# Cross-attention and a routed feed-forward: the context's key one group sooner, probabilities turned first, three heads divided on ScalarE

## The chip, the core and the metric

One core of one Trainium2 chip. The metric is the device time of one execution in microseconds (us).

## The reference

x is (8, 128, 256): 8 batch rows of 128 tokens. Each row goes through grouped attention with 16 query heads of width 128 over 4 key heads, with 128 context tokens put ahead of the row's own 128; then through a feed-forward with 8 experts, of which each token takes 2. Cut to the attention:

```python
q = rms_norm((x @ wq).reshape(B, L, 16, 128), q_norm_w)      # x here: layer-normed
k = rms_norm((x @ wk).reshape(B, L, 4, 128), k_norm_w)
k_ctx = rms_norm((h_ctx_kv @ wk_ctx).reshape(B, T, 4, 128), k_norm_w)   # no rotation
q = q * cos + rotate_half(q) * sin
k = k * cos + rotate_half(k) * sin
k_full = jnp.concatenate([k_ctx, k], axis=1)                  # values alike, without norm
probs = softmax(einsum('blhd,bmhd->bhlm', q, k_full) * scale + mask)
out = einsum('bhlm,bmhd->blhd', probs, v_full).reshape(B, L, 2048) @ wo
x = x + out
```

## The kernel before

The kernel walks over the 8 rows b, and inside a row over 4 groups g of 4 heads, one per key head. Row 0 and row 7 are written out, rows 1 to 6 are a hardware loop. Every engine has its own function `row(b, first, last)` with its instructions in an order written by hand; engines meet through semaphores only. A step number is u = 4b + g. `ahead_of(b, g, n, last)` names the group n steps later, over the row's end.

Each product is taken in three fp16 terms, so each operand is stored as a high half (ScalarE, `copy`, L471) and a low half (VectorE, `low`, L929): the tiles `..._hi` and `..._lo`. A step goes through the engines so:

- TensorE `scores` (L1318, L1340) into `sc_ps`; VectorE `scores_max` (L991) and the bias `nbias` (L995); ScalarE `exps` (L566) into `probs`; VectorE the reciprocal `rden` (L1000) and `normalise` (L1003), which divides the 4 heads one by one.
- One step later TensorE turns `probs` by 8 products (`turn_probs`, L1351) into `pt_ps`; ScalarE and VectorE make its halves (`p_copy`, `p_low`); TensorE multiplies by the values (`mix`, L1361) into `o_ps`; then `o_copy` and `o_low`.
- The query is made two groups ahead: TensorE `q` (L1203) into `proj`; VectorE rotates it (L920, L922); GpSimd adds the two parts into `q_rot` (`q_add`, L795) and makes the inverse root of its mean square (`q_roots`, L747 and L749) from ScalarE's `q_squares` (L510). One group ahead TensorE turns it (`q_turn`, L1297) into the bank `turn`, and `q_copy` and `q_low` make its halves.

In group 0 the context's value (`vc`) and the value (`v`, through `turn`) of the row are projected. In group 1 the row before gets its output projection (`out_proj`, L1388, 48 products into `proj[0]`) and its residual (`residual`, L1013). In group 2 the next row's context key (`kc`, L1216, into `turn`) and key (`k`, L1203, into `proj[1]`) are projected, ScalarE takes their squares (`kc_squares`, `k_squares`), GpSimd their roots (`kc_roots`, `k_roots`) and scales the key (`k_scale`, L781); ScalarE scales the context's key (`kc_scale`). In group 3 both are turned (L1249, L1268) and their halves are made, ScalarE's in the midst of the exponentials. The next row's scores need both high halves at their start and both low halves (`k_ready`, `kc_ready`) before their third part, the four products with `kT_lo`. The context of the next row is split by `ctx_high` and `ctx_low` in group 0 and turned by a DMA from SP's queue.

The bank `turn` is shared by the turned query, the value, the context's key and the turned context's key; each waits until the one before has been read.

Row 0 also prepares the output weights: in group 1 GpSimd multiplies half of them by a scale (L843) after its query's root; ScalarE and VectorE split them (`wo_split`).

## Time and profile before

| | us |
|---|---|
| median of 3 runs | 361.87 (359.09 to 362.88) |
| the profiled execution | 362.58 |
| its span, first to last instruction | 360.80 |
| mean granted TensorE clock | 0.982 of full |

Rows are in microseconds from the span's start. PE is TensorE's products, PEld its weight loads, DVE VectorE, ACT ScalarE, POOL GpSimd. A timeline row gives start, duration, engine, line, operation, names and shapes, the count merged into it, and in brackets how long the engine had been idle and what ended that. Products are pipelined, so their durations overlap and the step from start to start is what one costs. On the other engines the start of the next instruction comes a little before the end of the last.

### The profile page before, as it was taken

The numbers are of one execution on the slowest core, as the hardware profiler recorded it, in microseconds if no ns is written. First come the engines' busy times: TensorE is split into PE (matmuls) and PEld (weight loads), VectorE is DVE, ScalarE is ACT, GpSimd is POOL, SyncE is SP. The second block draws the span as 40 slices with busy tenths as digits, with TensorE's granted clock in tenths as the row PEclk, the third lists the DMA queues.
The fourth block names the chain that finished last, engine by engine and source line by source line (L and its number), as shares of the span: only waits on it lengthen the run. The fifth ranks groups of instructions, "written<-read, shape, count | busy, mean of one in ns | idle before, by whom it ended". The sixth has DMA issues, their size and how long they took to land.

```text
span 360.8 us, 7355 instructions
## 1 busy us (share of the span) xinstructions
PE 327.0 (91%) x2250; PEld 219.6 (61%) x2254; DVE 314.5 (87%) x602; ACT 259.9 (72%) x910; POOL 166.7 (46%) x241
## 2 busy tenths in 40 slices
PE   6677869779999999999999999999999999999994
PEld 5253635447665856585667566756766587856452
DVE  1578999989999899999998999899989997875773
ACT  4577769666898599759974997498759875747541
POOL 4366465854375427443734443454436431054530
PEclk9998989989999999999999999999999999999998
DMA  5996300002007100710031001000000000044683
GB/s 172 344 287 226 54 0 0 3 0 45 0 1 174 44 0 0 182 36 1 0 73 29 0 0 29 15 0 0 15 15 0 3 2 0 2 83 94 132 162 115
DMA packets 42450, 21.07 MB, mean 58 GB/s; under 512 B 31672, under 2 KB 39872, under 8 KB 42432
## 3 DMA queue, kind: packets, MB, share of 16 engines
q1 hardware_dynamic: 42432, 20.86, 22.7%
q8 instruction: 8, 0.13, 0.2%
q14 instruction: 10, 0.08, 0.1%
HBM read 12.20 MB, written 1.05 MB: 37 GB/s over the span
## 4 chain that ended last, share of the span: by engine, by line
PE 40%; DVE 19%; ACT 19%; issue 11%; POOL 6%; DMA 2%; SPq 1%; DVEq 1%; ACTq 0%; POOLq 0%
PE proj L1388 10%; ACT probs L566 8%; PE pt_ps L1351 6%; DVE probs L1003 4%; PE o_ps L1361 4%; PE proj L1203 4%; PE turn L1297 4%; POOL q_rot L795 3%; DVE nmax L991 3%; PE sc_ps L1318 3%; DVE pT_lo L929 2%; ACT pT_hi L471 2%; DMA wq<-in_L_xattn_wq_dram 2%; ACT kc_junk L510 2%; ACT q_junk L510 2%
## 5 line engine op out<-in xcount | busy, mean ns | idle before, releaser
L566 ACT ACTIVATE probs<-sc_ps,nbias,q_r 128x256 f32<-128x256 f32 x128 | 71.0, 574 | 6.5 <-DVE nbias L995 6.0
L795 POOL TENSOR_TENSOR q_rot<-q_t 128x512 f32<-128x512 f32 x32 | 42.4, 1325 | 42.6 <-DVE q_t L922 41.8
L1003 DVE TENSOR_SCALAR probs<-probs,rden 128x256 f32<-128x256 f32 x128 | 51.0, 460 | 1.1
L510 ACT ACTIVATE q_junk<-proj 128x128 bf16<-128x128 f32 x128 | 34.3, 304 | 12.9 <-DVE q_t L922 12.9
L1203 PE MATMUL proj<-wq_hi,xT 128*128 128x512 f16 x128 | 39.0, 387 | 3.8 <-DVE wq_lo L913 3.4
L471 ACT ACTIVATE pT_hi<-pt_ps 128x512 f16<-128x512 f32 x64 | 34.8, 598 | 9.2 <-PE pt_ps L1351 9.2
L929 DVE SCALAR_TENSOR_TENSOR pT_lo<-pt_ps,pT_hi 128x512 f16<-128x512 f32 x64 | 40.9, 680 | 0.2 <-ACT pT_hi L471 0.2
L991 DVE TENSOR_REDUCE nmax<-sc_ps 128x4 f32<-128x1024 f32 x32 | 38.9, 1214 | 1.5 <-PE sc_ps L1340 1.5
L749 POOL TENSOR_TENSOR q_r<-q_me,power 128x4 f32<-128x4 f32 x32 | 34.5, 1077 | 2.5
L1351 PE MATMUL pt_ps<-ident,probs 128*128 128x128 f32 x256 | 33.3, 273 | 0.4 <-DVE probs L1003 0.3
L471 ACT ACTIVATE qT_hi<-turn 128x512 f16<-128x512 f32 x32 | 19.6, 613 | 18.2 <-PE turn L1297 18.2
L471 ACT ACTIVATE oT_hi<-o_ps 128x512 f16<-128x512 f32 x32 | 19.9, 621 | 16.9 <-PE o_ps L1361 16.9
L1388 PE MATMUL proj<-wo_lo,oT_hi 128*128 128x256 f16 x112 | 30.5, 273 | 0.0
L1388 PE MATMUL proj<-wo_hi,oT_hi 128*128 128x256 f16 x112 | 30.5, 273 | 0.0
L1388 PE MATMUL proj<-wo_hi,oT_lo 128*128 128x256 f16 x112 | 30.5, 273 | 0.0
L1351 PEld LDWEIGHTS pt_ps<-ident,probs 128*128 128x128 f32 x256 | 28.8, 141 | 1.1 <-DVE probs L1003 0.9
L510 ACT ACTIVATION_READ_ACCUMULATOR q_junk<-proj 128x1 f32 x128 | 29.3, 236 | 0.0
L1361 PE MATMUL o_ps<-pT_hi,v_hi 128*128 128x512 f16 x64 | 24.3, 380 | 4.8 <-DVE pT_lo L929 4.7
L1297 PE MATMUL turn<-ident,q_rot 128*128 128x128 f32 x128 | 20.0, 279 | 8.9 <-POOL q_rot L795 6.2
L566 ACT ACTIVATION_READ_ACCUMULATOR probs<-sc_ps,nbias,q_r 128x1 f32 x128 | 27.5, 215 | 0.0
L929 DVE SCALAR_TENSOR_TENSOR oT_lo<-o_ps,oT_hi 128x512 f16<-128x512 f32 x32 | 22.0, 686 | 5.3 <-ACT oT_hi L471 5.3
L1318 PE MATMUL sc_ps<-kT_hi,qT_hi 128*128 128x256 f16 x128 | 24.5, 273 | 0.9 <-ACT probs L566 0.5
(216 smaller groups left out, 866.2 us busy)
## 6 DMA issues: line engine op xcount, KB each, us to landing
wq<-in_L_xattn_wq_dram SPq DMA_DIRECT2D x4, 512.0 KB, 9.1
w<-in_L_ffn_w_dram SPq DMA_DIRECT2D x2, 1024.0 KB, 10.4
wq<-in_L_xattn_wo_dram SPq DMA_DIRECT2D x1, 2048.0 KB, 8.1
ctx_b<-in_ctx_dram SPq DMA_DIRECT2D x8, 128.0 KB, 2.3
out_dram<-x_all SPq DMA_DIRECT2D x4, 256.0 KB, 2.2
x_all<-in_x_dram SPq DMA_DIRECT2D x1, 896.0 KB, 12.4
wkc<-in_L_xattn_wk_ctx_dram SPq DMA_DIRECT2D x1, 512.0 KB, 4.4
wk<-in_L_xattn_wk_dram SPq DMA_DIRECT2D x1, 512.0 KB, 5.3
```

The lines of the kernel that those rows point to most:

```text
L471: return nc.scalar.activation(out_, in_, ACT.Copy, scale=scale)
L510: last = nc.scalar.activation(junk[:, head], bank[:, head], ACT.Square, scale=scale, accum_out=dst[:, h:h + 1])
L566: last = nc.scalar.activation(probs[:, h, :], sc_ps[:, h, :], ACT.Exp, bias=nbias[:, h:h + 1], scale=q_r[:, g, h:h + 1], accum_out=den[:, ...
L795: nc.gpsimd.tensor_tensor(q_rot[:], q_t1[:], q_t2[:], ALU.add).then_inc(q_added, 1)
L929: return nc.vector.scalar_tensor_tensor(out=lo, in0=src, scalar=scale, in1=hi, op0=ALU.mult, op1=ALU.subtract)
L991: nc.vector.tensor_reduce(nmax[:], sc_ps[:], AX_X, ALU.max, negate=True).then_inc(s_max, 1)
L1003: last = nc.vector.tensor_scalar(probs[:, h, :], probs[:, h, :], rden[:, h:h + 1], None, ALU.mult)
L1203: last = nc.tensor.matmul(bank[:], xT[:, a, c, :], w[:, c, cols], start=(n == 0), stop=(n == 3 * DC - 1))
L1318: nc.tensor.matmul(sc_ps[:, h, :], a[:, h * P:(h + 1) * P], w[:, g, :, :].rearrange("p a t -> p (a t)"), start=start, stop=False, skip_gro ...
L1351: last = nc.tensor.transpose(pt_ps[:, a, h * P:(h + 1) * P], probs[:, h, a * P:(a + 1) * P], ident[:])
L1361: last = nc.tensor.matmul(o_ps[:], v[:, a, g * P:(g + 1) * P], p[:, a, :], start=(a == 0 and i == 0), stop=(a == 1 and i == 2))
L1388: last = nc.tensor.matmul(proj[0][:, 0:D], o[:, h // R, (h % R) * P:(h % R + 1) * P], w[:, h, :], start=(h == 0 and i == 0), stop=(h == H ...
```

## The change

1. `kc(b + 1)`, the next row's context key, is issued by TensorE in the middle of the output projection of group 1 (in row 0: at the end of group 1), instead of in group 2. ScalarE's `kc_squares` and GpSimd's `kc_roots` move into group 1; `kc_scale` stands first in group 2. The query's turn of group 3 waits for the scaled context key (`kc_norm`); that of group 0 no longer does.
2. In groups 1 and 2 TensorE turns the probabilities ahead of the query; ScalarE and VectorE make the halves in the same order. In groups 0 and 3 the order stays.
3. `by_act = (1, 2, 0, 0)`: ScalarE divides the last head in group 0 and the last two in group 1 (`normalise_rest`), VectorE the others. `turn_probs` waits for both.
4. ScalarE's and VectorE's halves of the context's value and of the next context come earlier in group 0.
5. On GpSimd, `q_roots` of the next row's first query follows its `q_add` at once, ahead of `k_roots`; `q_add` in group 2 no longer has `kc_roots` ahead of it.

```diff
@@ -356,8 +357,13 @@
         shared_banks = (o_ps[:], turn[:])
         gate_ps = (proj[1][:, 0:TT * E], turn[:, 0:TT * E])
         xn2_banks = (proj[1][:], turn[:], sc_a, sc_b)
+        by_act = (1, 2, 0, 0)
         half_e = (slice(0, E // 2), slice(E // 2, E))
         wT_landed = 16 * 3 * len(half_e)
+
+        def act_normalised(b, g):
+
+            return 2 * b + g
 
         def token_turned(eng, k):
 
@@ -569,6 +575,13 @@
                         last.then_inc(s_exp_half, 1)
                 last.then_inc(s_exp, 1)
 
+            def normalise_rest(b, g):
+                u = G * b + g
+                act.wait_ge(s_rden, u + 1)
+                for h in range(R - by_act[g], R):
+                    last = copy(probs[:, h, :], probs[:, h, :], rden[:, h:h + 1])
+                last.then_inc(s_probs_act, 1)
+
             def p_copy(u):
                 act.wait_ge(p_turned, u + 1)
                 for a in range(2):
@@ -620,19 +633,29 @@
             def row(b, first, last):
                 for g in range(G):
                     u = G * b + g
-                    if ahead_of(b, g, 1, last):
+                    if g in (0, 3) and ahead_of(b, g, 1, last):
                         q_copy(*ahead_of(b, g, 1, last))
                     if g == 1 and first:
                         ln_high(b + 1)
+                    if g == 2 and not last:
+                        kc_scale(b + 1)
                     if g or not first:
                         p_copy(u - 1)
+                    if g in (1, 2):
+                        q_copy(b, g + 1)
                     exps(b, g, (kc_copy, k_copy) if g == 3 and not last else ())
                     if g == 1 and not first and not last:
                         ln_high(b + 1)
-                    if g == 2 and not last:
-                        kc_squares(b + 1)
+                    if g == 0:
+                        vc_copy(b)
+                    if g == 0 and not last:
+                        ctx_high(b + 1)
                     if ahead_of(b, g, 2, last):
                         q_squares(*ahead_of(b, g, 2, last))
+                    if g == 1 and not last:
+                        kc_squares(b + 1)
+                    if by_act[g]:
+                        normalise_rest(b, g)
                     if first and g == 3:
                         wo_split(3)
                     if g == 0:
@@ -640,17 +663,12 @@
                     if (g or not first) and not (g == 3 and last):
                         o_copy(u - 1, (g - 1) % G)
                     if g == 2 and not last:
-                        kc_scale(b + 1)
                         k_squares(b + 1)
                     if g == 2 and last:
                         act.wait_ge(t_sh2, 1)
                         copy(gateT[:].rearrange("p c e -> p (c e)"), proj[0][:, D:D + DC * E])
                         copy(sh2T[:], proj[0][:, 0:D]).then_inc(r_sh2, 1)
                         xn_copy(1)
-                    if g == 0:
-                        vc_copy(b)
-                    if g == 0 and not last:
-                        ctx_high(b + 1)
                     if first and g == 1:
                         wo_split(0)
                         wo_split(1)
@@ -823,13 +841,12 @@
                         q_add(*ahead_of(b, g, 2, last))
                     if g == 0 and first:
                         ln_root(b + 1)
-                    if g == 2 and not last:
-                        kc_roots(b + 1)
                     if ahead_of(b, g, 2, last):
                         if g in (1, 2) and not first:
                             q_add(*ahead_of(b, g, 2, last))
-                        if g != 2:
-                            q_roots(*ahead_of(b, g, 2, last))
+                        if g == 1 and not last:
+                            kc_roots(b + 1)
+                        q_roots(*ahead_of(b, g, 2, last))
                     if g == 0 and not first and not last:
                         ln_root(b + 1)
                     if g == 1 and not first:
@@ -837,7 +854,6 @@
                     if g == 2 and not last:
                         k_roots(b + 1)
                         k_scale(b + 1)
-                        q_roots(b + 1, 0)
                     if first and g == 1:
                         pool.wait_ge(d_wo, 16)
                         nc.gpsimd.tensor_tensor(wo32[:, own_wo, :], wo32[:, own_wo, :],
@@ -999,7 +1015,7 @@
                 dve.wait_ge(s_exp, u + 1)
                 nc.vector.reciprocal(rden[:], den[:]).then_inc(s_rden, 1)
                 dve.wait_ge(s_rden, u + 1)
-                for h in range(R):
+                for h in range(R - by_act[g]):
                     last = nc.vector.tensor_scalar(probs[:, h, :], probs[:, h, :], rden[:, h:h + 1], None, ALU.mult)
                 last.then_inc(s_probs, 1)
 
@@ -1060,12 +1076,14 @@
                         wo_split(0)
                     if first and g == 0:
                         split_low(wv32[:], wv_hi[:], wv_lo[:], G + 2)
-                    if ahead_of(b, g, 1, last):
+                    if g in (0, 3) and ahead_of(b, g, 1, last):
                         q_low(*ahead_of(b, g, 1, last))
+                    if g or not first:
+                        p_low(u - 1)
+                    if g in (1, 2):
+                        q_low(b, g + 1)
                     if g == 1 and not first and not last:
                         ln_scale(b + 1)
-                    if g or not first:
-                        p_low(u - 1)
                     if g == 2 and not first:
                         second_norm(b - 1)
                     if ahead_of(b, g, 2, last):
@@ -1091,14 +1109,13 @@
                         wc_split(1)
                     if g == 0:
                         v_low(b)
+                        vc_low(b)
+                    if g == 0 and not last:
+                        ctx_low(b + 1)
                     if g or not first:
                         o_low(u - 1, (g - 1) % G)
                     if g == 2 and not last:
                         k_add(b + 1)
-                    if g == 0:
-                        vc_low(b)
-                    if g == 0 and not last:
-                        ctx_low(b + 1)
 
             row(0, True, False)
             with dve.Fori(1, B - 1) as b:
@@ -1236,7 +1253,7 @@
                     pe.wait_ge(cT_ready, 1)
                 else:
                     pe.wait_ge(d_cT, 16 * nb)
-                    pe.wait_ge(q_ready, G * nb)
+                    pe.wait_ge(q_ready, G * nb - 1)
                     pe.wait_ge(wc_low, 1)
                 project_ctx(nb, turn, wkc, wkc_hi, wkc_lo, kc_proj)
 
@@ -1284,15 +1301,18 @@
             def q_turn(b, g, last=False):
                 pe.wait_ge(q_added, G * b + g + 1)
                 if g == 0:
-                    pe.wait_ge(kc_norm, b + 1)
                     if isinstance(b, int) and b == 0:
                         pe.wait_ge(kc_ready, 1)
+                    else:
+                        pe.wait_ge(q_ready, G * b)
                 if g == 1:
                     pe.wait_ge(kc_ready, b + 1)
                 if g == 2:
                     pe.wait_ge(v_ready, b + 1)
                 if g == 3:
                     pe.wait_ge(q_ready, G * b + g)
+                    if not last:
+                        pe.wait_ge(kc_norm, b + 2)
                 for h in range(R):
                     last_ = nc.tensor.transpose(turn[:, h * P:(h + 1) * P], q_rot[:, h * P:(h + 1) * P], ident[:])
                 last_.then_inc(q_turned, 1)
@@ -1345,6 +1365,8 @@
 
                 u = G * b + g - 1
                 pe.wait_ge(s_probs, u + 1)
+                if by_act[(g - 1) % G]:
+                    pe.wait_ge(s_probs_act, act_normalised(b, g))
                 seen(pe, p_ready, 2 * u)
                 for a in range(2):
                     for h in range(R):
@@ -1376,12 +1398,14 @@
                 if g == G - 1:
                     last.then_inc(wo_done, 1)
 
-            def out_proj(b):
+            def out_proj(b, final):
                 pe.wait_ge(o_ready, G * b + G - 1)
                 pe.wait_ge(q_sq, G * b + G + 3)
                 pe.wait_ge(wo_low2, 1)
                 pe.wait_ge(wo_low, 2)
                 for h in range(H):
+                    if h == H // 2 and not final:
+                        kc(b + 2)
                     if h == H - R:
                         pe.wait_ge(o_ready, G * b + G)
                     for i, (o, w) in enumerate(((oT_hi, wo_hi), (oT_hi, wo_lo), (oT_lo, wo_hi))):
@@ -1455,10 +1479,12 @@
                 for g in range(G):
                     u = G * b + g
                     scores(b, g)
-                    if ahead_of(b, g, 1, last):
+                    if g in (0, 3) and ahead_of(b, g, 1, last):
                         q_turn(*ahead_of(b, g, 1, last), last)
                     if g or not first:
                         turn_probs(b, g)
+                    if g in (1, 2):
+                        q_turn(b, g + 1, last)
                     if first and g < 2:
                         pe.wait_ge(w_lo, g + 4)
                     if ahead_of(b, g, 2, last):
@@ -1467,7 +1493,6 @@
                         kc_turn(b + 1)
                         k_turn(b + 1)
                     if g == 2 and not last:
-                        kc(b + 1)
                         k(b + 1)
                     if g == 0:
                         vc(b)
@@ -1478,7 +1503,9 @@
                         v(b)
                     if g == 1:
                         if not first:
-                            out_proj(b - 1)
+                            out_proj(b - 1, last)
+                        else:
+                            kc(1)
                         pe.wait_ge(vc_ready, b + 1)
                         pe.wait_ge(v_ready, b + 1)
                     if g == 2 and last:
```

## Rows read from the trace of the kernel before

**Rows 1.** Part 1 of the page: busy time, share of the span, instructions.
```profile
PE 327.0 (91%) x2250; PEld 219.6 (61%) x2254; DVE 314.5 (87%) x602; ACT 259.9 (72%) x910; POOL 166.7 (46%) x241
```
**Rows 2.** Busy time per stretch; this one is one row of the loop.
```profile
core 0: us, PE busy (x) PEld busy (x) DVE busy (x) ACT busy (x) POOL busy (x), PEclk, DMA share, GB/s
...
183.19:218.27 35.08, 33.76 (x241) 23.34 (x240) 33.69 (x68) 27.81 (x108) 15.77 (x24) 1.00 0.05 11
```
**Rows 3.** Timeline of TensorE in that row: start, duration, what, idle before.
```profile
184.67 0.22 PE L1340 MATMUL sc_ps<-causal,identb 128*128 128x128 bf16 x1
185.37 0.63 PE L1297 MATMUL turn<-ident,q_rot 128*128 128x128 f32 x4 [0.48 <-DVE v_lo L929]
...
188.00 0.27 PE L1388 MATMUL proj<-wo_hi,oT_hi 128*128 128x256 f16 x1
...
193.24 0.38 PE L1361 MATMUL o_ps<-pT_hi,v_hi 128*128 128x512 f16 x1
...
194.53 0.38 PE L1318 MATMUL sc_ps<-kT_hi,qT_hi 128*128 128x256 f16 x2
...
198.68 1.46 PE L1216 MATMUL turn<-wk,cT 128*128 128x512 f16 x6
199.97 0.59 PE L1203 MATMUL proj<-wk_hi,xT 128*128 128x512 f16 x2
...
204.80 0.65 PE L1297 MATMUL turn<-ident,q_rot 128*128 128x128 f32 x4 [0.54 <-POOL q_rot L795]
...
208.29 0.66 PE L1268 MATMUL proj<-ident,k_rot 128*128 128x128 f32 x4 [0.24 <-POOL k_rot L781]
...
211.19 0.27 PE L1318 MATMUL sc_ps<-kT_lo,qT_hi 128*128 128x256 f16 x1
```
**Rows 4.** Timeline of VectorE in the same row.
```profile
186.68 1.21 DVE L991 TENSOR_REDUCE nmax<-sc_ps 128x4 f32<-128x1024 f32 x1
...
191.51 2.21 DVE L1003 TENSOR_SCALAR probs<-probs,rden 128x256 f32<-128x256 f32 x4
...
195.36 0.69 DVE L929 SCALAR_TENSOR_TENSOR oT_lo<-o_ps,oT_hi 128x512 f16<-128x512 f32 x1 [0.50 <-ACT oT_hi L471]
196.27 1.22 DVE L991 TENSOR_REDUCE nmax<-sc_ps 128x4 f32<-128x1024 f32 x1 [0.21 <-PE sc_ps L1340]
...
201.14 1.14 DVE L1003 TENSOR_SCALAR probs<-probs,rden 128x256 f32<-128x256 f32 x4
...
204.04 1.17 DVE L980 TENSOR_TENSOR k_sum<-k_t 128x512 f32<-128x512 f32 x1
205.14 1.21 DVE L991 TENSOR_REDUCE nmax<-sc_ps 128x4 f32<-128x1024 f32 x1
...
210.12 0.68 DVE L929 SCALAR_TENSOR_TENSOR kT_lo<-proj,kT_hi 128x512 f16<-128x512 f32 x1
```
**Rows 5.** Timeline of ScalarE: a probability copy and an exponential of group 2.
```profile
197.58 0.60 ACT L471 ACTIVATE pT_hi<-pt_ps 128x512 f16<-128x512 f32 x1 [0.28 <-PE pt_ps L1351]
...
198.55 0.57 ACT L566 ACTIVATE probs<-sc_ps,nbias,q_r 128x256 f32<-128x256 f32 x1
```
**Rows 6.** Timeline of GpSimd: the rotated query, in groups 1 and 2.
```profile
191.51 1.27 POOL L795 TENSOR_TENSOR q_rot<-q_t 128x512 f32<-128x512 f32 x1
...
203.40 1.26 POOL L795 TENSOR_TENSOR q_rot<-q_t 128x512 f32<-128x512 f32 x1
```
**Rows 7.** Timeline of GpSimd in row 0, groups 1 and 2.
```profile
46.20 4.26 POOL L843 TENSOR_TENSOR wq<-wq,scale_w 128x2048 f32<-128x2048 f32 x1
53.54 1.26 POOL L795 TENSOR_TENSOR q_rot<-q_t 128x512 f32<-128x512 f32 x1 [3.09 <-DVE q_t L922]
```
**Rows 8.** Timeline of VectorE in row 0, group 2.
```profile
48.76 1.71 DVE L995 TENSOR_TENSOR nbias<-nmax,q_r 128x4 f32<-128x4 f32 x1
...
53.58 2.16 DVE L1003 TENSOR_SCALAR probs<-probs,rden 128x256 f32<-128x256 f32 x4
```
**Rows 9.** Timeline of TensorE: row 0 group 2, and the last row.
```profile
51.17 2.72 PE L1216 MATMUL turn<-wk,cT 128*128 128x512 f16 x6 [2.87 <-issue]
...
290.44 0.63 PE L1297 MATMUL turn<-ident,q_rot 128*128 128x128 f32 x4 [0.23 <-DVE v_lo L929]
```

More of the change, by code:

```diff
@@ L305, in xattn_moe_kernel @@
         s_probs = sem("s_probs")
+        s_probs_act = sem("s_probs_act")
         p_turned = sem("p_turned")
```

## The prediction

> **What bounds the kernel now.** I read the page's busy shares first [rows 1]: TensorE is busy for 91% of the span and VectorE for 87%, so neither share names the limit. Next came the busy time of one whole row of the loop [rows 2]. Of its 35.08 us TensorE is busy for 33.76, VectorE for 33.69 and ScalarE for 27.81. There are six such rows. Two engines that are both nearly full hand the lead to each other, so the rest is read from timelines: who waits for whom, and at which place.
>
> TensorE [rows 3]: it runs from the first scores of group 1 (183.19) to those of group 2 (194.53) with one stall. Scores end at 184.73, 0.06 after the row of 184.67, and the query's turn starts at 185.37, held by VectorE's v_lo: 0.64 idle. In groups 2 and 3 it stalls three times more: about 0.7 ahead of the turn at 204.80 (0.54 by the row, which counts from a modelled end), 0.4 ahead of the key's turn at 208.29, and some 0.2 inside the next scores.
>
> VectorE [rows 4]: it idles where group 1 ends, 0.50 for the output's high half and 0.21 for the scores of group 2. From the maximum at 196.27 to the key's low half (210.12, ending at 210.80) it works almost without a break: 14.53 us. TensorE needs that low half for the third part of the next scores, which starts at 211.19, so VectorE has 0.39 to spare there. The row is therefore a loop of two legs. **TensorE's leg** goes from the third part of scores 0 to the end of scores 2. **VectorE's leg** goes from the maximum of group 2 to the key's low half. TensorE's stalls of groups 2 and 3 lie beside VectorE's leg and are not lost time.
>
> **The change, part by part, in a loop row.** (1) *The context's key moves from group 2 into the output projection of group 1.* It is 6 products, 198.68 to 199.97: 1.29 us [rows 3]. It leaves group 2, where TensorE has room, and enters TensorE's leg: +1.29. I expect no stall ahead of it. It would start at 184.73 + 0.87 + 0.44 + 1.30 + 2.62 = 189.96 (turned probabilities, turned query, projection, half of the output projection of 188.00 to 193.24). The low half of the query that it waits for comes by about 189.9: the maximum of group 1 at 186.68 as before, 1.34 to the bias, two probability halves (1.21) and 0.60. The margin is about zero, so 0 to 0.3 per row stays in the range. The transfer of the turned context starts about 0.7 earlier than before, since its split is moved ahead.
>
> (2) *Probabilities are turned ahead of the query.* They don't need v_lo, and VectorE's division ends before the scores do. The 0.64 goes: −0.64. TensorE's leg thus changes by 1.29 − 0.64 = **+0.65**.
>
> (3) *ScalarE divides 1 head of group 0 and 2 of group 1.* VectorE saves 3 x 0.27, a quarter of the free division of four heads at 201.14 (1.14 with its tail, [rows 4]). But in group 0 its next step waits for ScalarE's v_hi, which is queued behind the moved copy and the division, and in group 1 it already idles for TensorE. So the saving ends as more idle time. What ScalarE needs for one the trace doesn't show: between 0.3 (half of its 512-wide copy of 0.60) and 0.57 (its exponential of the same 256 columns) [rows 5]. I take 0.38, as a copy does no sum, 1.1 in all. ScalarE is idle for 7.3 us of the row [rows 2], and the turns that wait for its last head come some 2 us later. I take 0 for both.
>
> (4) *GpSimd adds the rotated query of group 2 at once, instead of behind the key's mean square.* This is the costly edit. Before, GpSimd held q_rot until 203.40, where it made k_sum wait: k_sum took 1.10 from start to start against 0.60 when alone [rows 4, 6]. Now q_rot starts as soon as the second half of the rotation is there, and so does the division, one reciprocal later. Wherever the two start together, the division's four heads take 2.21 instead of 1.14 (at 191.51) [rows 4, 6]. Row 0 of the kernel already has this very order in group 2: q_rot at 53.54, division at 53.58 for 2.16 [rows 7, 8]. So +1.07 for the division, −0.50 for k_sum. VectorE now takes the probabilities' low half ahead of the query's, 1.34 after the maximum; ScalarE's high half of it starts 0.2 (the maximum's own lag behind the scores) less than 0.87 + 0.2 after that maximum and takes 0.60 (the copy at 197.58, [rows 5]), so it is there at 1.5 and VectorE waits: +0.20. Sum of VectorE's leg: 1.07 − 0.50 + 0.20 = **+0.77**.
>
> The Trainium skill (SBUF — State Buffer, "SBUF: two separate sides") says that GpSimd and a VectorE instruction of this kind share a port pair which "starts first gets the pair for the whole instruction". The waits of 1.07 agree. By that rule alone it would matter who is first: if the division won all four times, it would lose nothing and the sum would be 1.07 per row less. That is a rival below.
>
> A loop row changes by 0.65 + 0.77 less the 0.39 to spare: **+1.03**. Six rows: +6.2. A check by VectorE's own time: 35.08 less 0.71 idle is 34.37 of work, waits for GpSimd in it; less 0.81 and plus 0.57 that is 34.1. It leaves some 2.0 idle at the end of group 1: the 0.71 of before, 0.65 for TensorE's longer leg, 0.54 for the two heads that it no longer divides there. 36.1 against 35.1.
>
> **Row 0.** There the context's key is projected at the end of group 1 at about 43.5, once its input has been turned and the low half of query 2 is there. ScalarE's squares of it then end at 46.5 to 47.3. GpSimd takes the key's root (1.35) and then the query's (1.25) ahead of its scaling of the output weights, which before started at 46.20 and took 4.26 [rows 7]. It starts at 49.2 to 50.1 now and ends at 53.4 to 54.3. Before, its end held up VectorE's bias, 1.71 instead of 0.16, until 50.47 [rows 8]. The maximum would end at about 50 to 50.8, inside the scaling, so the bias would wait until its end: +3.0 to +3.8. TensorE's idle time ahead of the context's key (2.87, [rows 9]) goes, but VectorE's chain runs beside it. I take +3.0. If the bias slips in before the scaling starts, it is −1.6 instead.
>
> **Last row.** No context key; the query's turn at 290.44 stood 0.39 idle: −0.4.
>
> **Sum.** 6.2 + 3.0 − 0.4 = +8.8. The profiled execution took 362.58 (span 360.80), so 371.4 for it; it lies 0.7 above the median of the runs, 361.87, from which the same sum gives **370.7**.
>
> **Rivals.** *The division wins the port (18%).* q_rot starts by 0.04 us first in row 0 [rows 7, 8] and at the same 10 ns in the loop; a shift of a few hundredths would turn it round, though a head alone is 0.27 and q_rot could still come between two. Then VectorE's leg changes by −0.30, and the row by 0.65 − 0.30 − 0.39, about 0. With row 0 and the last: 361.87 + 2.6 = 364.5.
>
> *Row 0 does not lose (10%).* The bias gets through ahead of the scaling. The sum is 6.2 − 1.6 − 0.4: 366.1.
>
> *VectorE's work doesn't end the loop (10%), faster.* If TensorE alone sets the row, all four stalls (0.64 + 0.70 + 0.40 + 0.23) could go, but VectorE's 34.1 of work stops it at −1.0 per row: 361.87 − 6.0 − 0.4 = 355.5. It decides from the point at which VectorE's leg is under 14.53 + 0.39 − 0.65 = 14.27 us. For it speak the stalls that the moved normalisation removes; against it, that VectorE works those 14.53 us with no gap to close, and that none of the moved divisions lies in it.
>
> *The change does nothing that lasts (10%).* The parts cancel: the leg of VectorE keeps its length, the moved key is paid by the stall that goes. 361 to 364.
>
> **Numbers.** Forecast 52% (368 to 373). The bounds of the unknown costs are 0 to 0.3 per row for the wait ahead of the moved key, −1.07 to 0 for the port, −1.6 to +3.8 in row 0. The range takes in the two middle rivals: 364 to 373.5. About 1% is what a measurement of this kernel can tell from no change. Slower by over 1% (above 365.5): the forecast, the second rival and under half of the first, 0.70. Within 1%: the rest of the first and nearly all of the last, 0.19. Faster: the third and a little of the last, 0.11.
>
> **What would show it.** In the profile after: a loop row of about 36.1 (35.08 before); six more products inside the output projection, and the mix behind it ending some 0.65 later against the scores of group 1; VectorE idle for about 2 us in group 1, with its wait for the output projection as a new line; the first head of the division in group 2 at about 1.4 us instead of 0.35, q_rot beside it; k_sum at 0.7 instead of 1.17; TensorE waiting for k_lo or k_rot in group 3. In row 0, the bias of group 2 ends at 53 or later. The forecast is wrong if the maximum of group 2 to the key's low half takes no longer than 14.3 us, or if VectorE doesn't idle at the end of group 1.

## The result, and the profile after

| | before | after |
|---|---|---|
| median of 6 runs, us | 361.48 (359.09 to 362.88) | 373.98 (371.65 to 374.73) |
| the profiled execution | 362.58 | 374.73 |
| its span | 360.84 | 373.01 |

The ratio is 1.037, interval 1.033 to 1.041: 12.5 us slower. The forecast was slower too, by 8.8 us: 370.7 in a range that ended at 373.5, half a microsecond under the measured median.

I cut the span at the starts of VectorE's maximum of group 0, one per row. "A loop row" below is the distance of two such starts, as read for row 5 unless said otherwise; the medians of the runs stand beside it.

| part of the span, us | before | after | difference | forecast |
|---|---|---|---|---|
| start to row 0 | 28.73 | 28.36 | −0.37 | 0 |
| row 0 | 39.70 | 42.00 | +2.30 | +3.0 |
| row 1 | 39.09 | 39.72 | +0.63 | +1.03 |
| rows 2 to 6 | 175.49 | 184.43 | +8.94 | +5.2 |
| row 7 and the end | 77.82 | 78.50 | +0.68 | −0.4 |

So the five steady rows hold nearly all that was missed. The busy time of one of them (the windows view; columns as in [rows 2]):

```profile
220.72:257.62 36.90, 34.76 (x243) 22.95 (x242) 33.58 (x65) 28.95 (x110) 15.90 (x24) 1.00 0.05 11
```

The row is 36.90 long where [rows 2] had 35.08. VectorE is busy for 33.58 of it (33.69 before), so it now idles 3.32 where it idled 1.39. TensorE has the same products; its busy time, whose ends are modelled, is 1.00 longer. TensorE's timeline of that row, where the moves can be seen:

```profile
229.10 0.63 PE L1317 MATMUL turn<-ident,q_rot 128*128 128x128 f32 x4
229.61 0.60 PE L1220 MATMUL proj<-wq_hi,xT 128*128 128x512 f16 x2
...
233.43 0.27 PE L1412 MATMUL proj<-wo_hi,oT_lo 128*128 128x256 f16 x1
233.71 1.47 PE L1233 MATMUL turn<-wk,cT 128*128 128x512 f16 x6
235.02 0.27 PE L1412 MATMUL proj<-wo_hi,oT_hi 128*128 128x256 f16 x1
...
250.36 0.61 PE L1220 MATMUL proj<-wq_hi,xT 128*128 128x512 f16 x2 [1.27 <-ACT k_junk L516]
252.25 0.66 PE L1266 MATMUL turn<-ident,kc_n 128*128 128x128 f32 x4 [0.42 <-DVE qT_lo L945]
```

The context's key stands in the middle of the output projection: 233.71 to 235.02 is 1.31, and 0.17 of waiting lies ahead of it (0.28 from the start of the product before it, which costs 0.11). In group 2, which the context key's products have left, TensorE now idles 1.27 until ScalarE has taken the squares of the key; that place lies beside VectorE's leg. VectorE's timeline:

```profile
225.74 1.52 DVE L1019 TENSOR_SCALAR probs<-probs,rden 128x256 f32<-128x256 f32 x3
...
228.26 0.69 DVE L945 SCALAR_TENSOR_TENSOR v_lo<-turn,v_hi 128x512 f16<-128x512 f32 x1 [0.92 <-ACT v_hi L477]
228.87 0.68 DVE L945 SCALAR_TENSOR_TENSOR v_lo<-proj,v_hi 128x512 f16<-128x512 f32 x1
...
237.96 0.42 DVE L1029 SCALAR_TENSOR_TENSOR x_all<-proj,x_all 128x256 f32 x1 [1.03 <-PE proj L1412]
...
239.76 0.69 DVE L945 SCALAR_TENSOR_TENSOR oT_lo<-o_ps,oT_hi 128x512 f16<-128x512 f32 x1 [0.56 <-ACT oT_hi L477]
240.67 1.23 DVE L1007 TENSOR_REDUCE nmax<-sc_ps 128x4 f32<-128x1024 f32 x1 [0.21 <-PE sc_ps L1360]
...
242.18 1.29 DVE L945 SCALAR_TENSOR_TENSOR pT_lo<-pt_ps,pT_hi 128x512 f16<-128x512 f32 x2
...
245.70 2.17 DVE L1019 TENSOR_SCALAR probs<-probs,rden 128x256 f32<-128x256 f32 x4
...
249.58 0.68 DVE L996 TENSOR_TENSOR k_sum<-k_t 128x512 f32<-128x512 f32 x1
```

Three things answer to [rows 4]. The division of group 2 takes 2.17 where it took 1.14, and GpSimd's q_rot starts 0.04 ahead of it:

```profile
245.66 1.27 POOL L813 TENSOR_TENSOR q_rot<-q_t 128x512 f32<-128x512 f32 x1 [4.78 <-DVE q_t L938]
```

k_sum takes 0.68 instead of 1.17. And at the end of group 1 VectorE idles 1.80 in three pieces (1.03, 0.56, 0.21), the first of them new. What the prediction had not put a price on is the 0.92 ahead of v_lo. ScalarE's timeline tells where it is from:

```profile
225.41 0.60 ACT L477 ACTIVATE v_hi<-proj 128x512 f16<-128x512 f32 x1 [0.67 <-PE o_ps L1383]
225.91 0.41 ACT L477 ACTIVATE cT<-ctx_b 128x256 f16<-128x256 f32 x1
226.21 0.27 ACT L516 ACTIVATE q_junk<-proj 128x128 bf16<-128x128 f32 x1
...
227.21 0.53 ACT L477 ACTIVATE probs<-probs,rden 128x256 f32<-128x256 f32 x1
227.61 0.62 ACT L477 ACTIVATE v_hi<-turn 128x512 f16<-128x512 f32 x1
```

The moved copy of the context's value may not overwrite v_hi before the mix has read it, so it waits 0.67 with the query's squares, the division and the value's own copy queued behind it.

In lengths of the two legs of the prediction, row 5: TensorE's leg 19.96 before and 21.46 after, VectorE's 14.52 and 15.18, VectorE's spare time ahead of the third part of the scores 0.40 and 0.06. 1.50 + 0.66 − 0.34 = 1.82, which is the 36.90 − 35.08. The spare time is what the legs leave of a row, with 0.2 from the end of scores 2 to VectorE's maximum; where it grows, something other than VectorE holds the next scores.

### The profile page after: what moved, and what is told of

Its sections match the earlier page's. It is cut to its first block and busy times, and to the rows that moved or that the text cites. A ratio compares the mean times of both kernels' runs of the same rounds, so it can differ in the third digit from the quotient of the medians.

```text
span 373.0 us, 7378 instructions
## 1 busy us (share of the span) xinstructions
PE 332.5 (89%) x2254; PEld 217.6 (58%) x2254; DVE 313.2 (84%) x578; ACT 269.1 (72%) x934; POOL 166.6 (45%) x241
## 5 line engine op out<-in xcount | busy, mean ns | idle before, releaser
L767 POOL TENSOR_TENSOR q_r<-q_me,power 128x4 f32<-128x4 f32 x32 | 33.5, 1045 | 2.5
L1373 PEld LDWEIGHTS pt_ps<-ident,probs 128*128 128x128 f32 x256 | 27.5, 141 | 5.2 <-issue 4.3
L1383 PE MATMUL o_ps<-pT_hi,v_hi 128*128 128x512 f16 x64 | 25.2, 394 | 2.8 <-DVE pT_lo L945 2.8
L516 ACT ACTIVATION_READ_ACCUMULATOR q_junk<-proj 128x1 f32 x128 | 27.6, 216 | 0.0
L1383 PE MATMUL o_ps<-pT_lo,v_hi 128*128 128x512 f16 x64 | 25.3, 395 | 0.0
L1383 PE MATMUL o_ps<-pT_hi,v_lo 128*128 128x512 f16 x64 | 25.3, 395 | 0.0
```

What stands on the lines that cost most here:

```text
L516: last = nc.scalar.activation(junk[:, head], bank[:, head], ACT.Square, scale=scale, accum_out=dst[:, h:h + 1])
L1373: last = nc.tensor.transpose(pt_ps[:, a, h * P:(h + 1) * P], probs[:, h, a * P:(a + 1) * P], ident[:])
L1383: last = nc.tensor.matmul(o_ps[:], v[:, a, g * P:(g + 1) * P], p[:, a, :], start=(a == 0 and i == 0), stop=(a == 1 and i == 2))
```

## The experiments

All kernels are before or after with parts put in or taken out. One table for the outcomes; every ratio is against runs of before on the same chip.

| kernel | median, us | ratio (interval) | loop row | TensorE's leg | VectorE's leg |
|---|---|---|---|---|---|
| before | 361.5 | | 35.08 | 19.96 | 14.52 |
| after | 373.98 | 1.037 (1.033 to 1.041) | 36.90 | 21.46 | 15.18 |
| a_kcback: after, key in its old place | 365.66 | 1.015 (1.007 to 1.023) | 35.68 | 19.70 | 15.20 |
| a_nodiv: after, ScalarE divides none | 369.38 | 1.028 (1.020 to 1.037) | 36.49 | 21.06 | 15.17 |
| a_oldg0: after, group 0 in the old order | 370.39 | 1.029 (1.021 to 1.037) | 36.38 | 20.95 | 15.17 |
| a_kturn: after, key rotated ahead of the division | 370.63 | 1.030 (1.022 to 1.038) | 36.59 | 21.45 | 14.88 |
| b_kc: before, key moved | 373.33 | 1.031 (1.028 to 1.035) | 37.02 | 21.33 | 15.40 |
| b_tp: before, probabilities first | 367.28 | 1.016 (1.011 to 1.021) | 35.77 | 19.75 | 15.20 |
| b_tp1: the same in group 1 alone | 358.75 | 0.991 (0.988 to 0.994) | 34.87 | 19.74 | 14.53 |
| a_both: key moved, probabilities first | 367.89 | 1.018 (1.014 to 1.021) | 36.53 | 21.10 | 15.18 |
| c_p34: before, division and order of group 0 | 365.16 | 1.015 (1.009 to 1.021) | 35.63 | 20.51 | 14.52 |
| c_vc: b_tp1, value's halves together | 356.81 | 0.986 (0.980 to 0.993) | 34.51 | 19.37 | 14.53 |
| c_vc_d2: and 1 head of group 2 on ScalarE | 358.00 | 0.995 (0.992 to 0.999) | 34.75 | 19.37 | 14.57 |
| c_vc_d12: and 2 of group 1 | 357.53 | 0.993 (0.990 to 0.996) | 34.71 | 19.37 | 14.55 |

The row is the surer column: from row 2 on it repeats within 0.1 us inside an execution, where the medians carry 2 to 3 us of row 0 (last section). Each row comes from one profiled execution. c_vc's median has the widest runs behind it, 353.0 to 359.9.

### Parts taken out of after

**a_kcback.**

```diff
+        if g == 2 and not last: kc(b + 1)   # TensorE, group 2
-        if h == H // 2 and not final: kc(b + 2)      # in the output projection
```

The cut shows TensorE's lines alone; ScalarE's squares and scaling, GpSimd's roots and the waits go back to group 2 with them.

> The changed kernel with the context's key, its squares, its root and its scaling back in group 2 (GpSimd's order there is that of before too); the turned probabilities first, the divisions on ScalarE and the earlier halves in group 0 stay. Theory A (the moved key costs 1.29 us on TensorE's leg, the collision of the division of group 2 with q_rot 0.5 on VectorE's): the loop row falls from 36.9 to 34.8 to 35.1, total 359 to 362. Rival B (the divisions and copies moved on ScalarE delay the value and set the row): the row stays at 36 or more, total over 368.

365.66 us. The loop row falls by 1.22 to 35.68: the moved key is most of the loss in a row. But the row is not that of before, as my theory had it, nor the 36 of the rival; there is something else that costs 0.6. b_tp below finds it.

**a_nodiv.**

```diff
-        by_act = (1, 2, 0, 0)
+        by_act = (0, 0, 0, 0)
```

> The changed kernel with by_act all zero: VectorE divides all heads, all else is as changed. Theory A: the value's high half comes 0.4 us earlier in group 0 (one division of 0.40 less ahead of it), which takes away up to 0.4 of TensorE's waits in group 1, and VectorE's 0.27 more per head falls into its idle time: row 36.4 to 36.8, total 371 to 374. Rival B: row under 36, total under 368.

The row falls by 0.41, all of it in TensorE's leg, as expected; the median of 369.38 is under the 371 to 374. In the profiled execution row 0 is 3.0 shorter than after's, which the theory had left out. ScalarE's division, costed at nothing, costs here, where it stands behind the moved copy and ahead of the value's copy. A division itself takes ScalarE 0.40, from 227.21 to the next start at 227.61 above.

**a_oldg0.**

```diff
+                    if g == 0:
+                        vc_copy(b)                   # ScalarE: behind v_copy and o_copy again
-                        vc_low(b)                    # VectorE: behind o_low again
```

The cut shows one line for each engine; both halves of the context's value, and the next context's with them, go back on both.

> The changed kernel with the halves of the context's value and of the next context back at the end of group 0, on ScalarE and VectorE. Theory A: ScalarE's copy of the context's value waits for the mix of the step before, and pushes the query's squares from 0.7 to 1.7 us behind the rotation and the value's high half with them. Back in its place it gives up to 0.4 per row (0.24 ahead of the query's turn, 0.17 ahead of the context's key): row 36.4 to 36.6, total 370.5 to 372.5. Rival B: row under 36. If the order was harmless: row 36.9, 374.

The row falls by 0.52, in TensorE's leg alone, just under the 36.4 to 36.6. Yet taking both out (a_both) leaves 36.53, no less than either alone: TensorE's leg is 21.10 with neither, 21.06 with the new order alone, 20.95 with the division alone, and 21.46 with both. With the key moved and the probabilities first, neither part costs anything by itself; together their delays of the value's high half add up, the wait for the mix and then the division. And even both together cost nothing with the probabilities first and the key in group 2: a_kcback is b_tp with parts 3 and 4, and its row is 35.68 against 35.77. So their price belongs to the combination: 0.55 on before (c_p34), 0 on b_tp, 0.36 on a_both. The query's product behind the turn starts 8.57 behind the maximum of group 0 in a_nodiv, 8.58 in a_oldg0 and 8.89 in after.

**a_kturn.**

```diff
+                    if g == 2 and not last: k_turn(b + 1)     # VectorE, two rotations
                     normalise(b, g)
-                    if g == 2 and not last: k_turn(b + 1)
```

> The changed kernel with VectorE's rotation of the key ahead of the division in group 2, so that q_rot on GpSimd is done before the division starts. Theory A: the division takes 1.14 instead of 2.17 and the key's squares come 2 us earlier; VectorE's leg gets 0.9 to 1.0 shorter and so does the row: 35.9 to 36.1, total 367.5 to 369.5. Rival C (TensorE alone sets the row since the key was moved): row stays at 36.8 or more, 373 to 374.

VectorE's leg falls by only 0.30 and the row by 0.31, between my theory and the rival. VectorE's timeline and GpSimd's:

```profile
244.08 1.15 DVE L1015 TENSOR_SCALAR probs<-probs,rden 128x256 f32<-128x256 f32 x4
...
247.60 0.88 DVE L1007 TENSOR_TENSOR nbias<-nmax,q_r 128x4 f32<-128x4 f32 x1
```

```profile
242.85 1.27 POOL L809 TENSOR_TENSOR q_rot<-q_t 128x512 f32<-128x512 f32 x1 [4.80 <-DVE q_t L934]
...
247.42 1.04 POOL L795 TENSOR_TENSOR k_rot<-k_sum,k_r 128x512 f32<-128x512 f32 x1
```

The 1.02 of the division goes, which shows that the collision with q_rot was the whole of it. But 0.72 comes back at once in the bias, which now meets k_rot: it starts 0.18 after it and ends with it (0.88 where it takes 0.16). The Trainium skill (SBUF — State Buffer, "SBUF: two separate sides") has the engine that comes first hold the shared port pair for its whole instruction. These rows agree: an instruction of 128 x 4 elements waited for one of 128 x 512.

### Parts added to before

**b_kc.** The key's move alone, GpSimd's order with it.

```diff
+                    if h == H // 2 and not final: kc(b + 2)
-                        kc(b + 1)
```

Again TensorE's lines alone.

> The kernel before with the context's key alone moved into group 1 (with its squares, root and scaling, and GpSimd's earlier q_add and root of group 2 that follow from it); the query is still turned first, no head on ScalarE, group 0 as before. Theory A: 1.29 on TensorE's leg and 0.5 on VectorE's, less the 0.4 that VectorE had to spare: row 36.4 to 36.6 (35.1 before), and row 0 over 2 us longer: total 370 to 373, about the whole loss. Rival D (the loss needs the moved order of turned probabilities or the divisions): row under 35.8, total under 366.

373.33 us, ratio 1.031: this edit alone costs nearly as much as the whole change, and in a row of the loop more (37.02 against 36.90; I had expected 36.4 to 36.6). It puts +1.37 on TensorE's leg (its six products take 1.29 to 1.31) and +0.88 on VectorE's. The long division and VectorE's new wait for the output projection are there in full:

```profile
234.69 2.19 DVE L1002 TENSOR_SCALAR probs<-probs,rden 128x256 f32<-128x256 f32 x4
238.03 0.42 DVE L1012 SCALAR_TENSOR_TENSOR x_all<-proj,x_all 128x256 f32 x1 [1.15 <-PE proj L1392]
...
246.00 2.16 DVE L1002 TENSOR_SCALAR probs<-probs,rden 128x256 f32<-128x256 f32 x4
```

The division and k_sum make 0.54 of VectorE's 0.88. The other 0.34 has no term in the prediction. The query's turn of group 3 writes into `turn`, where the projected context key now lies until ScalarE has scaled it. The turn starts 0.14 behind the maximum of group 2, where before had it 0.20 ahead; both halves of the query and of the probabilities move with it:

```profile
240.88 0.66 PE L1299 MATMUL turn<-ident,q_rot 128*128 128x128 f32 x4 [0.18 <-ACT kc_n L471]
```

**b_tp.** Probabilities ahead of the query in groups 1 and 2, on all three engines (TensorE's lines are shown).

```diff
-                    if ahead_of(b, g, 1, last):
+                    if g in (0, 3) and ahead_of(b, g, 1, last):
                         q_turn(*ahead_of(b, g, 1, last), last)
                     if g or not first: turn_probs(b, g)
+                    if g in (1, 2): q_turn(b, g + 1, last)
```

> The kernel before with the probabilities turned ahead of the query in groups 1 and 2, nothing else. Theory A: TensorE's 0.6 of group 1 goes; but in group 2 the context's key now waits for the query's low half, which VectorE makes 1.2 later, about 1.1 of idle on TensorE, and in the last row the turn of the normed tokens waits alike: row 34.8 to 35.2, total 360 to 362.5. Rival E (turning probabilities first is a plain gain): row 34.5, total 358 or less.

A loop row of 35.77 and a median of 367.28, longer than before and outside both expectations. TensorE's leg is 0.21 shorter, but in group 2:

```profile
235.97 0.68 DVE L931 SCALAR_TENSOR_TENSOR qT_lo<-turn,qT_hi 128x512 f16<-128x512 f32 x1
```

```profile
236.75 1.46 PE L1220 MATMUL turn<-wk,cT 128*128 128x512 f16 x6 [0.92 <-issue]
```

The context's key writes into the bank `turn`, and there it waits for the query's low half, which now comes behind the probabilities'. The key, its squares and its scaling come later, ScalarE's copy of the output behind them, and VectorE's leg is 0.68 longer. The spare time grows by 0.22 as well, since the key's turn has to wait for GpSimd's k_rot. This is the 0.6 left over in a_kcback, which has the same legs. Added to before, part 2 costs 0.69; added to b_kc it takes 0.49 off the row (a_both, 36.53), 0.23 on TensorE's leg and 0.22 on VectorE's, where it hides b_kc's wait for the scaled key. So in group 2 it seems worth having only where the key isn't there; b_kc with group 1 alone swapped was not run.

**b_tp1.** The same with `g in (1,)`.

> The kernel before with the probabilities turned ahead of the query in group 1 only, where the value's low half holds the query. Theory A: the stall of 0.6 on TensorE's leg goes and nothing waits in group 2: row 34.4 to 34.6, total 357.5 to 359, faster than before. Rival F (VectorE's total work of 34.4 sets the row, not the leg): row 34.9 to 35.1, total 361.

34.87, the first that beats before: ratio 0.991. It lies between my theory and the rival F. The stall of 0.64 ahead of the query's turn is gone, yet the row is only 0.21 shorter. What is late next:

```profile
217.71 0.60 PE L1301 MATMUL turn<-ident,q_rot 128*128 128x128 f32 x4
218.51 0.60 PE L1207 MATMUL proj<-wq_hi,xT 128*128 128x512 f16 x2 [0.20 <-DVE v_lo L931]
```

```profile
217.18 0.68 DVE L931 SCALAR_TENSOR_TENSOR oT_lo<-o_ps,oT_hi 128x512 f16<-128x512 f32 x1
217.78 0.68 DVE L931 SCALAR_TENSOR_TENSOR v_lo<-proj,v_hi 128x512 f16<-128x512 f32 x1
```

The next product of the query goes into the bank that holds the context's value, and waits until VectorE has made its low half (217.78 + 0.68 = 218.46). From the turn's start to the product's it is 0.80 where four turns cost 0.44: 0.36 of the 0.64 is back. Rival F falls with c_vc below, where the row drops to 34.51 with no work taken from VectorE.

**a_both.** After without parts 3 and 4, or: b_kc and b_tp together.

> The changed kernel without the divisions on ScalarE and with the halves of group 0 in their old places: the moved key and the turned probabilities alone. Theory A: all of TensorE's waits behind ScalarE's queue in group 0 are gone, and the row is what the prediction's sum for the key and the turn gives, 36.1 to 36.3; total 368 to 370. If the two undone edits add up (0.4 and 0.5): 36.0.

A row of 36.53, over the 36.1 to 36.3 that I expected. Against b_kc TensorE's leg is 0.23 shorter: part 2 is worth 0.2 here as in b_tp1, not 0.64. Against after it is 0.36 shorter: that is what parts 3 and 4 cost in this change. The places: in after the query's product starts 8.89 behind the maximum of group 0 (229.61 − 220.72), in a_both 8.71, and a_both has none of the 0.17 ahead of the key.

**c_p34.** Parts 3 and 4 alone on before.

> The kernel before with the other two parts of the change alone: ScalarE divides one head of group 0 and two of group 1, and in group 0 the context value's copy and the context's halves stand ahead of the query's squares (ScalarE) and ahead of the output's low half (VectorE). The context's key and the order of the turns stay as before. Theory (these two parts delay the value's halves, since the context value's copy waits for the mix ahead of the squares): the value's low half comes some 0.7 us later in a row than before, and the turn of the query, which waits for it, with it: a loop row of 35.7 to 36.0 us where before has 35.1, a ratio of 1.010 to 1.02, 365 to 369 us where before has 361.5. Rival (they cost nothing, as the prediction had it): a row of 35.0 to 35.2 us, 360 to 362.5 us.

A row of 35.63, 0.55 longer, just under what I expected; the rival of no cost is out. Where the query's turn still stands first, the whole delay falls on it:

```profile
219.70 0.69 DVE L940 SCALAR_TENSOR_TENSOR v_lo<-turn,v_hi 128x512 f16<-128x512 f32 x1 [0.70 <-ACT v_hi L473]
```

```profile
220.54 0.63 PE L1307 MATMUL turn<-ident,q_rot 128*128 128x128 f32 x4 [0.95 <-DVE v_lo L940]
```

1.11 of stall by the starts, where [rows 3] had 0.64.

### A version faster than both

**c_vc.** b_tp1, and the context value's halves right behind the value's on both engines. Part 4 of the change moved this copy too, but ahead of the squares, where it waits 0.67 for the mix; here it stands behind the value's copy and waits for nothing.

```diff
 ScalarE                    if g == 0:
                                v_copy(b)
+                               vc_copy(b)
 VectorE                    if g == 0:
                                v_low(b)
+                               vc_low(b)
                            if g or not first:
                                o_low(u - 1, (g - 1) % G)
```

> The kernel before with the probabilities turned first in group 1 only, and in group 0 the context value's high and low half made right behind the value's own, ahead of the output's halves (on ScalarE and on VectorE). Theory (with the turns swapped in group 1 alone, the next product of the query waits 0.36 us for the context value's low half, and this order gives it back): row 34.4 to 34.6 us where the swap alone has 34.87 and before 35.1; ratio 0.980 to 0.989, 355 to 357.5 us where before has 361.5. Rival (the output's low half, now later, holds up the output projection, or VectorE is what ends group 1): row 34.8 to 34.95, 358 to 359.5 us.

```profile
216.17 0.67 DVE L930 SCALAR_TENSOR_TENSOR v_lo<-proj,v_hi 128x512 f16<-128x512 f32 x1
216.76 0.67 DVE L930 SCALAR_TENSOR_TENSOR oT_lo<-o_ps,oT_hi 128x512 f16<-128x512 f32 x1
```

```profile
216.70 0.60 PE L1299 MATMUL turn<-ident,q_rot 128*128 128x128 f32 x4
217.13 0.59 PE L1205 MATMUL proj<-wq_hi,xT 128*128 128x512 f16 x2
```

The product now follows the turn with no wait (0.43), as expected. The row is 34.51, down by 0.36 from b_tp1 and by 0.57 from before, and the median 356.81, ratio 0.986. The output projection, for which the output's low half now comes 0.6 later, doesn't wait.

**c_vc_d2**, `by_act = (0, 0, 1, 0)`, and **c_vc_d12**, `by_act = (0, 2, 1, 0)`, on top of it:

> As the kernel with the context value's halves sooner, and ScalarE divides one head of four in group 2, where VectorE's leg (maximum of group 2 to the key's low half) stands between the key's rotation and its end. Theory (VectorE's leg sets the second half of the row, and loses one division of 0.3 us): row 34.1 to 34.3 us, 353.5 to 356 us. Rival (ScalarE's head delays the scaling of the context's key and the key's squares, which stand behind it, and so the key's turn): row 34.5 to 34.9 us, 356.5 to 359.5 us.

> As the one before, and ScalarE divides two heads of group 1 as well, where it is idle some 1.9 us and VectorE's first head meets GpSimd's sum of the query (2.16 us for four heads). Theory (in group 1 TensorE's leg is the one that ends last, so VectorE's shorter division moves nothing): the same row as with one head of group 2 alone, within 0.1 us. Rival (once the stall of group 1 is gone VectorE ends it): 0.1 to 0.4 us a row shorter than with one head of group 2 alone.

The rival held for the head of group 2. In c_vc_d2 VectorE's division is 0.26 shorter, but VectorE then waits for ScalarE, whose copy of the output stands behind its own head, and its leg ends no sooner (14.57 against 14.53):

```profile
231.83 0.88 DVE L1015 TENSOR_SCALAR probs<-probs,rden 128x256 f32<-128x256 f32 x3
...
234.53 0.69 DVE L941 SCALAR_TENSOR_TENSOR oT_lo<-o_ps,oT_hi 128x512 f16<-128x512 f32 x1 [0.62 <-ACT oT_hi L473]
```

The row is 0.24 longer than without, and VectorE's spare time takes most of that (0.62 where c_vc has 0.40). What comes late is the key's turn, 12.30 behind the maximum of group 2 where c_vc has 12.03, and the next scores with it. GpSimd's mean square of the key waits for ScalarE's squares, which stand behind ScalarE's own head, and k_rot waits for that:

```profile
239.25 0.66 PE L1281 MATMUL proj<-ident,k_rot 128*128 128x128 f32 x4 [0.41 <-POOL k_rot L793]
```

Two heads of group 1 change 0.04, as expected: VectorE is not the one who ends that group.

## Why the prediction missed

The direction, the two legs, the cost of the moved key and the collision of the division with q_rot were right. What failed is the sum of TensorE's leg, at two steps: "The 0.64 goes" for part 2, and "I take 0 for both" for parts 3 and 4. Together they make 0.77 of the 0.79 that a row came out too long.

- **TensorE's leg, +0.65 forecast, +1.50 measured.** The moved key was right: +1.29 forecast, +1.37 measured (b_kc), of which some 1.3 are its products. The 0.17 of waiting ahead of it in after lay in the 0 to 0.3 that was left open; a_both has none of it, so it belongs to parts 3 and 4. The prediction had worked out its margin of zero with the maximum of group 1 "as before"; it came 9.68 behind that of group 0 (230.40 − 220.72), where before has 8.91.
- **Part 2, −0.64 forecast, −0.23 measured** (a_both against b_kc). The step "They don't need v_lo, and VectorE's division ends before the scores do. The 0.64 goes" was right about that stall and stopped there. It didn't ask what is late next: the query's product behind it needs the context value's low half, 0.36 later (b_tp1; c_vc takes it away).
- **Parts 3 and 4, "I take 0 for both", +0.36 measured** (after against a_both; +0.55 alone in c_p34). The price of one head, 0.38 forecast and 0.40 measured, was right, as was that VectorE's saving ends as idle time. The step that failed is that nothing hangs on that idle time. VectorE's 0.92 stands ahead of v_lo, and three things on TensorE come late one behind the other: the query's turn waits for v_lo (228.26 + 0.69), its product for the context value's low half (228.87 + 0.68), and the moved key for the query's low half, which VectorE makes behind them. The prediction named v_lo as the holder of TensorE's stall in its first part, saw that v_hi is queued behind the moved copy and the division, and didn't join the two. Nor does it say that the moved copy waits for the mix. The 0.36 is the price in this change and not one of the parts: with the key in group 2 and the probabilities first it is 0 (a_kcback against b_tp).
- **VectorE's leg, +0.77 forecast, +0.66 measured.** Division +1.03 (forecast +1.07), k_sum −0.49 (−0.50). The leg's further term, the low half of the probabilities first, came out near the forecast +0.20: from the maximum to the query's rotation it is 3.63 in after and 3.47 in c_vc, which has the old order there. The spare time of 0.39 was used up but for 0.06. The forecast was near in part because part 2 is there: without it the moved key costs this leg 0.34 more (b_kc), which the prediction had not seen.
- **The rival of the port** didn't come: q_rot started 0.04 ahead of the division, the same small lead as in row 0 of before. In a_kturn, where the two don't meet, the gain of 1.02 was real and 0.72 of it was lost to the next collision.
- **Row 0, +3.0 forecast, +2.30 measured.** The bias of group 2 started at 50.30 and ended at 53.05, behind GpSimd's scaling of the output weights, as the prediction had it. The scaling started at 49.43, inside the forecast 49.2 to 50.1, but took 3.60 and not the 4.26 of [rows 7], so it ended at 53.03 and not at 53.4 to 54.3:

```profile
50.30 2.75 DVE L1011 TENSOR_TENSOR nbias<-nmax,q_r 128x4 f32<-128x4 f32 x1
```

```profile
49.43 3.60 POOL L859 TENSOR_TENSOR wq<-wq,scale_w 128x2048 f32<-128x2048 f32 x1
```

- **Last row, −0.4 forecast, +0.68 measured.** The change also turns the order of the halves in the last row's group 2, and there a turn of the normed rows into the bank `turn` waits for the query's low half, which now comes second. Before has no such wait at that place. b_tp has this order too and b_tp1 not, and from row 7 to the end b_tp takes 78.33 and b_tp1 77.60. The stall of 0.39 that was to go gave 0.2 (77.60 against 77.82), as in the rows of the loop.

```profile
316.04 0.65 PE L1438 MATMUL turn<-ident,xn_all 128*128 128x128 f32 x4 [1.15 <-DVE qT_lo L945]
```

- **The account.** Rows 1 to 6 brought 3.4 more than forecast, the last row 1.1 more, row 0 0.7 less and the start 0.4 less: 3.4, the distance from +8.8 to the +12.2 of the spans. Of the 0.79 that row 5 brought more, part 2 makes 0.41 on TensorE's leg, parts 3 and 4 0.36, and the three small ones (the key +0.08, VectorE's leg −0.11, the spare time +0.05) 0.02. This goes by legs in after. Built up part by part the shares are others, since the parts act on each other: the key alone costs 1.94 and not 1.47 (1.29 + 1.07 − 0.50 − 0.39), and part 2 on top gives back 0.49, near the forecast −0.64 + 0.20.
- **"Parts cancel", "row 0 does not lose"** didn't come. In a_nodiv the bias did get through, ahead of the scaling that started at 49.05, and row 0 took 39.02:

```profile
48.44 0.16 DVE L996 TENSOR_TENSOR nbias<-nmax,q_r 128x4 f32<-128x4 f32 x1
```

That its edit did this is not shown: in after the granted clock was 0.50 from 44.5 to 47.5, right ahead of that place, and in a_nodiv it was 1.00 there.
- **The signs that it had named for being wrong** didn't come either: VectorE's leg is 15.18, not under 14.3, and VectorE idles 1.80 at the end of group 1 (forecast about 2). Both look at VectorE, and the miss lies in TensorE's leg.

What stays open: row 1 grew by 0.63 only, against 1.8 in the rows behind it. It differs from them in every kernel (39.1 before) and I didn't take it apart. Some 1.6 of its length can be clock: the granted clock of row 1 is 0.96 in before and after and 1.00 in a_kturn and c_vc_d12, where row 1 takes 38.16 and 37.53. That doesn't explain the 0.63, as before and after have the same. How much of a kernel's row 0 is its order and how much its clock is open too (next section).

## What to carry to other kernels

When a stall goes, the gain is the distance to the next thing that is late there, so list what the next two instructions of that engine wait for before booking it: here 0.64 was worth 0.2 until the second wait was moved as well, and then 0.57. Work moved to an engine with idle time is free only if what is queued behind it, and releases the critical engine, can still come later: 0.4 of division on a ScalarE with 7 idle microseconds cost 0.4 of the row where the value's copy behind it was late already (after against a_nodiv), and nothing where it wasn't (a_oldg0 against a_both). So measure such a part in the combination in which it will run. And room in an engine's queue belongs to a place: TensorE had time for the context's key in group 2 and none in group 1.

## What the runs showed of the hardware

A GpSimd instruction with its operands in SBUF held up a small VectorE instruction that came behind it until it was done: the bias of 128 x 4 elements, 0.16 alone, took 2.75 beside the scaling of 128 x 2048 and 0.88 beside k_rot. Not every instruction is held: in before the output's low half, which reads a PSUM bank, took 0.69 at 203.43, inside q_rot's 203.40 to 204.66. A move of order took 1.02 off the division and put 0.72 on the next such instruction (a_kturn).

TensorE's granted clock fell to the lower of its two levels (1.2 instead of 2.4 GHz, a granted 0.50) at different places in kernels with the same code up to there. In before it is 0.50 from 31.0 to 33.5, just behind 1.96 of idle time ahead of the query's turn that opens row 0. b_tp1 has the same 1.96 there and stays at 1.00; its fall came earlier, 0.50 from 14.5 to 17.5, and began inside an idle time of 2.69 that ended at 14.77; before idled 3.37 at that place and stayed at 1.00. The windows view, the stretches 0 to 28 and 28 to 37, of before and then of b_tp1:

```profile
0.00:28.00 28.00, 18.87 (x172) 13.48 (x172) 14.46 (x19) 14.93 (x46) 12.94 (x38) 1.00 0.78 259
28.00:37.00 9.00, 7.04 (x26) 3.46 (x26) 7.54 (x14) 6.93 (x27) 5.74 (x6) 0.81 0.71 233
```

```profile
0.00:28.00 28.00, 20.33 (x172) 14.34 (x172) 14.56 (x19) 15.49 (x49) 13.57 (x38) 0.94 0.79 259
28.00:37.00 9.00, 7.46 (x47) 4.94 (x48) 8.86 (x18) 7.44 (x26) 6.71 (x11) 1.00 0.69 233
```

A granted 0.81 over 9 us and 0.94 over 28 us are each about 1.7 us of clock: the same loss, once inside row 0 and once ahead of it. Over the whole of row 0, before and then a_both:

```profile
28.73:68.43 39.70, 32.98 (x191) 19.64 (x192) 37.18 (x65) 32.44 (x113) 23.79 (x27) 0.91 0.23 64
```

```profile
27.95:64.98 37.03, 29.33 (x191) 18.72 (x192) 35.68 (x66) 32.43 (x113) 24.84 (x28) 1.00 0.22 69
```

As an estimate from these, the lower clock can have cost before's row 0 up to 3.6 us (39.70 x 0.09), after's 3.4 (0.92), b_tp1's 1.9 (0.95) and a_both's nothing. By this measure the +2.30 of row 0 between before and after owes little to the clock, though the falls lie at different places. Of what b_tp1's 37.90 and a_both's 37.03 are below before's 39.70, up to 1.7 and 3.6 us may be clock and not their edits. Only the rows of the loop from row 2 on, at a granted 1.00 in all kernels, were compared for small differences.
